# Edge stage of a four-layer tower: compares for the next one-hots ahead of the picking, softmax pieces behind it, fetched columns laid out place by place

## Chip, cores and metric
One Trainium2 chip, one of its cores. The metric is the device time of one launch in microseconds (us), median of several executions.

## The reference
The program is a tower of four layers over 16384 tokens of 64 features (float32). The change lies in the graph attention of layer 2, which the reference writes so:

```
h = (x_flat @ W_gat).reshape(M, HEADS, NUM_EXPERTS)        # M = 16384 nodes, 4 x 4 = 16 columns
a_src = (h * att_src).sum(-1)
a_dst = (h * att_dst).sum(-1)
e = leaky_relu(a_src[src] + a_dst[dst], negative_slope=0.2)  # 262144 edges and one loop per node
e_max = segment_max(e, dst)
ee = exp(e - e_max[dst])
denom = segment_sum(ee, dst)
msg = h[src] * (ee / denom[dst])[:, :, None]
agg = segment_sum(msg, dst) + b_gat
```

Everything else of the tower (embeddings, three other attentions, four expert layers) is the same in both kernels.

## The kernel before
The edges lie sorted by destination, 2048 to each of the 128 partitions. `edge_softmax` walks them in 32 chunks of 64 edges per partition and keeps a running softmax along each partition's row. For every edge it needs the 16 columns of `h[src]` and four logits. It gets them in two ways: 36 of the 64 edges of a chunk come by indirect DMA (POOL, L2875), and 28 are fetched by TensorE. These 28 are handled in 7 groups of 4 edges; one edge place on all 128 partitions is called a tile here.

A fetched group goes through four steps:

- **Compares** (`prepare`, DVE, L2961). Four `tensor_scalar` build a one-hot matrix for the group in `hot_room`, which has two slots. They read lanes that SP's queue loads ahead (`columns`, L2836).
- **Matmuls** (PE, `fetch`, L2887). Per tile 8 matmuls of 512 columns write one of 4 banks in PSUM. A tile waits until the bank's last content, 4 tiles earlier, was copied out (`fetched_in`). The 512 columns hold 32 candidate places times 16 channels.
- **Copy** (ACT, `take`, L2907). One copy per tile from the bank to `fetched` in SBUF, which has two slots, too. It waits until the slot's last group was picked (`selected`).
- **Picking** (`select`, DVE, L2978 to L2983). Five halvings by the low bits of the source: `copy_predicated` over 1024, 512, 256 and 128 elements, a copy and a last `copy_predicated` of 64.

Beside them each chunk has softmax pieces. `maxima` (DVE, L2989 to L3017) does the destination logits, the source logits of the fetched edges (a product into `inp_s`, L3002, and its sum, L3004), the running maximum and the differences. `exps` (ACT, L2912 to L2914) takes three exponentials of them. `sums` (DVE, L3021 to L3026) scales the values and runs the sums in one scan. `states` (ACT, L2920 to L2922) copies the chunk's results by time into `GT`, from where SP's queue stores them. `low_bits` (L2956) makes the masks for a whole chunk; before the change it stands inside `maxima`.

The order of the work is written out by hand, a loop of instructions per engine, with semaphores between engines. While chunk c has its softmax, the fetched groups of chunk c+1 pass. DVE's order for one chunk is: `maxima(c)`, `select` of group 0 of c+1, compares of group 2, `sums(c)`, then for groups 1 to 6 `select` and the compares two groups on. ACT's order is: copies of group 0, `exps(c)`, copies of groups 1 and 2, `states(c)`, copies of groups 3 to 6.

Of the kernel before, what the change touches and what calls it, by code (L numbers as in the profile page):

```python
# [2583 lines left out]
BLOCKS = 4  # L2584
# [193 lines left out]
def edge_softmax(nc, g, q, att_src):  # L2778
# [7 lines left out]
    with Stage(nc, "edges") as st:  # L2786
# [16 lines left out]
        parts = g.part_room[:].rearrange("p (s b c u) -> p s b c u", s=PARTS, b=BLOCKS, c=CH)  # L2803
        fetched = g.XT[:, TOKENS // 2:TOKENS // 2 + 2 * PER_GROUP * WIDE].rearrange(
            "p (s t c u) -> p s t c u", s=2, t=PER_GROUP, c=CH)
        whole = g.XT[:, TOKENS // 2:TOKENS // 2 + TILES * CH].rearrange("p (b c u) -> p b c u", b=BLOCKS, c=CH)
# [8 lines left out]
        (split, numbered, powers, att_in, hot_ready, bank_full, fetched_in, halved, selected, pe_passed, act_passed, dve_passed) = (  # L2815
            st.sem(n) for n in ("split", "numbered", "powers", "att_in", "hot_ready", "bank_full", "fetched_in", "halved", "selected",
                                "pe_passed", "act_passed", "dve_passed"))
# [5 lines left out]
        with nc.Block() as block:  # L2823
# [56 lines left out]
            def _(pe):  # L2880
                def fetch(n, j, k):
                    wait_apart(pe, hot_ready, n * GROUPS + j + 1, pe_passed)
                    for t in range(PER_GROUP):
                        pe.wait_ge(fetched_in, n * ON_PE + j * PER_GROUP + t + 1)
                        for b in range(BLOCKS):
                            for p in range(PARTS):
                                m = nc.tensor.matmul(banks[t % BANKS][:], hot[:, (k * GROUPS + j) % 2, b, t, :],  # L2887
                                                     parts[:, p, b].rearrange("p c u -> p (c u)"),
                                                     start=b == 0 and p == 0, stop=b == BLOCKS - 1 and p == PARTS - 1)
# [9 lines left out]
            def _(act):  # L2899
# [3 lines left out]
                def take(n, j, k):  # L2903
                    wait_apart(act, selected, n * GROUPS + j + 1, act_passed)
                    for t in range(PER_GROUP):
                        act.wait_ge(bank_full, n * ON_PE + j * PER_GROUP + t + 1)
                        nc.scalar.copy(fetched[:, (k * GROUPS + j) % 2, t].rearrange("p c u -> p (c u)"),  # L2907
# [36 lines left out]
            def _(v):  # L2944
# [26 lines left out]
                def select(n, j, k):  # L2971
                    at = fetched[:, (k * GROUPS + j) % 2]
                    to = rows[:, k, BY_DMA + j * PER_GROUP:BY_DMA + (j + 1) * PER_GROUP, 0:CH]
                    taken = lambda s, w: bc(bc(bits[:, s, j * PER_GROUP:(j + 1) * PER_GROUP], 2, CH), 3, w)
# [8 lines left out]
                    vec.copy_predicated(to, bc(bits[:, LOW_BITS - 1, j * PER_GROUP:(j + 1) * PER_GROUP], 2, CH),  # L2983
                                        at[:, :, :, 1]).then_inc(selected, 1)

                def maxima(c, k, i, more):
# [53 lines left out]
                low_bits(0).then_inc(cleared, 1)  # L3040
                values = q.table[:, :, 0:CH].rearrange("p (b u) c -> p b c u", b=BLOCKS)
# [14 lines left out]
                v.wait_ge(cleared, 6)  # L3056
# [3 lines left out]
                v.wait_ge(cleared, 7)  # L3060
                prepare(0, 0, 0)
                prepare(0, 1, 0)
                for j in range(GROUPS):
                    select(0, j, 0)
                    ahead(0, j, 0)
# [287 lines left out]
```

## Time and profile before

| | |
|---|---|
| median of 3 runs | 7020.88 us (7016.52 to 7023.06) |
| profiled execution, its own time | 7022.01 us |
| span of that execution | 7020.3 us |
| busy in the span: PE, DVE, ACT, POOL | 5579.5, 5269.5, 2713.2, 1967.5 us |
| PE matmuls of the edge stage (L2887) | 7168, busy 1709.6 us |
| DVE picking (L2978, four forms) | 896, busy 662.2 us |
| DVE compares (L2961) | 896, busy 380.4 us |
| ACT copies (L2907) | 896, busy 520.1 us |

The page gives the busy time of each engine over the whole program; the edge stage is only the part from about 3340 to 5235 us. What its engines do in turn is read from the timelines of one chunk, some 59 us long, since the same pattern comes 31 times. In a timeline a row starts with its time from the start of the span; idle time before it and who ended it stand in brackets.

### The profile page before, as it was taken

The numbers are of one execution on the slowest core, as the hardware profiler recorded it, in microseconds if no ns is written. First come the engines' busy times: TensorE is split into PE (matmuls) and PEld (weight loads), VectorE is DVE, ScalarE is ACT, GpSimd is POOL, SyncE is SP. The second block draws the span as 40 slices with busy tenths as digits, with TensorE's granted clock in tenths as the row PEclk, the third lists the DMA queues.
The fourth block names the chain that finished last, engine by engine and source line by source line (L and its number), as shares of the span: only waits on it lengthen the run. The fifth ranks groups of instructions, "written<-read, shape, count | busy, mean of one in ns | idle before, by whom it ended". The sixth has DMA issues, their size and how long they took to land. (4 is left out here: it accounts for less than half of the span.)

```text
span 7020.3 us, 109468 instructions
## 1 busy us (share of the span) xinstructions
PE 5579.5 (79%) x41602; PEld 3506.8 (50%) x41668; DVE 5269.5 (75%) x8911; ACT 2713.2 (39%) x4310; POOL 1967.5 (28%) x1937
## 2 busy tenths in 40 slices
PE   4659888958639999960899999999970689689998
PEld 3552256622126666650777777777750258523332
DVE  7869977878878888860778877887772667677776
ACT  3534433434336666640333333333330332233332
POOL 0010010010047800007766666666636010100000
PEclk8869999979869999975999999999985899799999
DMA  0000000011121000000221221111111000000001
GB/s 16 1 6 1 25 17 22 8 35 37 55 32 15 19 2 2 2 35 14 37 35 35 37 38 38 37 38 38 38 29 11 1 3 3 17 1 1 1 1 25
DMA packets 152249, 141.18 MB, mean 20 GB/s; under 512 B 71746, under 2 KB 136420, under 8 KB 150052
## 3 DMA queue, kind: packets, MB, share of 16 engines
q1 hardware_dynamic: 98462, 115.20, 5.8%
q0 software_dynamic: 53376, 20.06, 3.6%
q8 instruction: 277, 4.54, 0.3%
q14 instruction: 122, 0.99, 0.0%
q10 hardware_dynamic: 12, 0.39, 0.0%
HBM read 62.80 MB, written 38.09 MB: 14 GB/s over the span
## 5 line engine op out<-in xcount | busy, mean ns | idle before, releaser
L2887 PE MATMUL edges_bank<-part_room,hot_room 128*128 128x512 f32 x7168 | 1709.6, 401 | 370.6 <-DVE hot_room L2961 368.0
L2887 PEld LDWEIGHTS edges_bank<-part_room,hot_room 128*128 128x128 f32 x7168 | 1389.1, 195 | 691.0 <-issue 373.0
L2875 POOL DMA_INDIRECT XT<-gat_node_table,edges_idx x1152 | 1194.7, 1037 | 656.5 <-issue 342.8
L2907 ACT COPY XT<-edges_bank 128x512 f32<-128x512 f32 x896 | 520.1, 593 | 1191.4 <-PE edges_bank L2887 1190.6
L2978 DVE COPY_PREDICATED XT<-edges_tabs_p,XT 128x1024 f32<-128x1024 int32 (+3 forms) x896 | 662.2, 739 | 328.5 <-ACT XT L2907 298.1
L1005 ACT ACTIVATE expd_act_out<-expd_hp 128x1024 f32<-128x1024 f32 x256 | 262.2, 1024 | 527.1 <-PE expd_hp L927 527.1
L1041 DVE TENSOR_TENSOR expd_act_out<-expd_act_out,expd_h 128x1024 f32<-128x1024 f32 x256 | 312.6, 1221 | 186.5 <-ACT expd_act_out L1005 185.6
L1459 ACT ACTIVATE GT<-attc_sc,attc_nm 128x256 f32<-128x256 f32 x1024 | 400.4, 481 | 36.2 <-DVE attc_nm L1525 36.2
L1473 ACT ACTIVATE GT<-attc_sct 128x1024 f32<-128x1024 f32 x256 | 262.4, 1025 | 325.9 <-PE attc_sct L1393 325.3
L2961 DVE TENSOR_SCALAR hot_room<-edges_lanes,edges_nodes 128x512 fp32r<-128x512 f16 x896 | 380.4, 487 | 0.0
L1524 DVE TENSOR_REDUCE attc_mx<-attc_sc 128x4 f32<-128x1024 f32 x256 | 313.3, 1224 | 87.3 <-PE attc_sc L1382 87.2
L1382 PE MATMUL attc_sc<-XT,attc_tT 64*128 64x256 f32 x2048 | 296.4, 409 | 45.4 <-ACT GT L1459 45.4
L1046 DVE TENSOR_TENSOR expd_hid<-expd_act_out,expd_gp 128x1024 f32<-128x1024 f32 x256 | 312.5, 1221 | 8.8
L1529 DVE TENSOR_REDUCE attc_rs<-GT 128x4 f32<-128x1024 f32 x256 | 310.1, 1211 | 1.3 <-ACT GT L1459 1.3
L927 PE MATMUL expd_hp<-XT,expd_in_w 64*128 64x512 f32 x1024 | 289.0, 641 | 3.3 <-PEq L82 2.0
L1403 PE MATMUL attc_op<-GT,attc_xB 128*64 128x256 f32 x2048 | 277.5, 391 | 7.2 <-ACT GT L1480 2.0
L959 PE MATMUL expd_yp<-expd_hid,expd_in_w 128*64 128x512 f32 x1024 | 276.8, 619 | 1.6 <-DVE expd_hid L1046 1.6
L505 POOL TENSOR_TENSOR ln_f_xn<-H,ln_f_mean 128x1024 f32<-128x1024 f32 x4 | 11.4, 2846 | 947.5 <-DVE ln_f_shift L542 947.5
L1393 PE MATMUL attc_sct<-attc_tT,XT 64*128 64x256 f32 x2048 | 267.0, 378 | 1.6 <-DMA attc_tT<-attc_rT 1.0
L927 PE MATMUL expd_h<-XT,expd_in_wg 64*128 64x512 f32 x1024 | 263.3, 591 | 0.2 <-DVE expd_act_out L1041 0.2
L1382 PEld LDWEIGHTS attc_sc<-XT,attc_tT 64*128 64x128 f32 x2048 | 185.6, 190 | 144.6 <-issue 116.8
L798 PE MATMUL gates_gt<-identb,GT 128*128 128x128 bf16 x64 | 6.3, 266 | 262.5 <-DVE GT L789 261.2
(774 smaller groups left out, 9936.4 us busy)
## 6 DMA issues: line engine op xcount, KB each, us to landing
edges_lanes<-gat_places SPq DMA_DIRECT2D x224, 128.0 KB, 3.1
gat_states<-GT SPq DMA_DIRECT2D x32, 768.0 KB
XT<-gat_node_table,edges_idx POOLq DMA_INDIRECT x1152
XT<-XT SPq DMA_DIRECT2D x32, 256.0 KB
XT<-XT SPq DMA_DIRECT2D x64, 128.0 KB
XT<-XT SPq DMA_DIRECT2D x128, 64.0 KB
gat_starts<-nodes_zeros SPq DMA_DIRECT2D x4, 1088.0 KB, 7.9
attb_q<-attb_rows SPq DMA_DIRECT2D x256, 2.0 KB
```

Source lines behind the costliest of these rows:

```text
L927: m = nc.tensor.matmul(bank[:, odd, :], w[half, e, :], g.XT[half, i * U:(i + 1) * U], start=True, stop=True)
L1041: nc.vector.tensor_tensor(act_out[:, u % 2], act_out[:, u % 2], h2[:], ALU.mult).then_inc(product_ready, 1)
L1046: nc.vector.tensor_tensor(hid[:, u % 2], act_out[:, u % 2], gp[:], ALU.mult).then_inc(hid_full, 1)
L1382: m = nc.tensor.matmul(sc[(0, 1, 1, 0)[hp]][:, n, a * S:(a + 1) * S], tT[half, b % NB, hp, a * P:(a + 1) * P], x(b, half), start=True, sto ...
L1459: m = nc.scalar.activation(prob[:, hp % 2, n, a, :], sc[(0, 1, 1, 0)[hp]][:, n, a * S:(a + 1) * S], ACT.Exp, bias=nm[:, b % 2, n, hp, a:a ...
L1524: link(vec.tensor_reduce(best, sc[(0, 1, 1, 0)[hp]][:].rearrange("p n (a s) -> p n a s", s=S), AX.X, ALU.max))
L1529: vec.reduce_sum(rs[:, b % 2, :, hp, :], prob[:, hp % 2], AX.X).then_inc(totaled, 1)
L2875: nc.gpsimd.indirect_dma_start(out=rows[:, k, c, :], out_offset=None, in_=q.t_table, in_offset=bass.IndirectOffsetOnAxis(ap=idx[:, k, c:c ...
L2887: m = nc.tensor.matmul(banks[t % BANKS][:], hot[:, (k * GROUPS + j) % 2, b, t, :], parts[:, p, b].rearrange("p c u -> p (c u)"), start=b = ...
L2907: nc.scalar.copy(fetched[:, (k * GROUPS + j) % 2, t].rearrange("p c u -> p (c u)"), banks[t % BANKS][:]).then_inc(fetched_in, 1)
L2961: m = vec.tensor_scalar(hot[:, (k * GROUPS + j) % 2, b], lanes[:, j], nodes[:, b:b + 1], None, ALU.is_equal)
L2978: vec.copy_predicated(at[:, :, :, 0:w], taken(s, w), at[:, :, :, w:2 * w]).then_inc(halved, 1)
```

## The change
DVE's order for one chunk becomes: compares of group 2 of c+1, `low_bits(c+1)`, `select` of group 0, `maxima(c)`, compares of group 3, `select` of group 1, `sums(c)`, then compares ahead of `select` for groups 2 to 6. Compares now wait for PE's matmuls of the group that had the slot (`bank_full`), which the picking did for them before. `low_bits` gets a semaphore of its own and a wait on it. On ACT the copies of group 1 go ahead of `exps(c)`; `states(c)` stays behind the copies of group 2. The fetched columns, and the tables that PE multiplies by, are laid out place by place (u, then c) in place of channel by channel (c, then u), so that each halving reads and writes runs of w x 16 elements in place of w. The product of L3002 goes to a contiguous `prod` in place of `inp_s`. The clearing of `halved` moves behind the last `copy_predicated`.

```diff
-        fetched = ... "p (s t c u) -> p s t c u", s=2, t=PER_GROUP, c=CH)
+        fetched = ... "p (s t u c) -> p s t u c", s=2, t=PER_GROUP, c=CH)
...
+        prod = g.XT[:, at + 2 * HEADS2 * W:at + 2 * HEADS2 * W + ON_PE * CH].rearrange("p (t h e) -> p t h e", h=HEADS2, e=PERH)
...
                 def during(c, k, i):
                     take(c + 1, 0, 1 - k)
+                    take(c + 1, 1, 1 - k)
                     exps(c)
-                    take(c + 1, 1, 1 - k)
                     take(c + 1, 2, 1 - k)
                     states(c, k, i)
...
                 def low_bits(c):
                     at = src_row[:, ds(c * C + BY_DMA, ON_PE)]
-                    return vec.tensor_tensor(bits, bc(at, 1, LOW_BITS), bc(pow2[:], 2, ON_PE), ALU.bitwise_and)
+                    v.wait_ge(selected, c * GROUPS + 2)
+                    vec.tensor_tensor(bits, bc(at, 1, LOW_BITS), bc(pow2[:], 2, ON_PE), ALU.bitwise_and).then_inc(bits_ready, 1)
+                    v.wait_ge(bits_ready, c + 1)
 
                 def prepare(n, j, k):
+                    if not (isinstance(n, int) and n == 0 and j < 2):
+                        v.wait_ge(bank_full, n * ON_PE + (j - 1) * PER_GROUP)
                     v.wait_ge(lanes_in[j], 16 * n + 16)
...
-                        vec.copy_predicated(at[:, :, :, 0:w], taken(s, w), at[:, :, :, w:2 * w]).then_inc(halved, 1)
+                        vec.copy_predicated(half(0, w), taken(s, w), half(w, 2 * w)).then_inc(halved, 1)
                         v.wait_ge(halved, s + 1)
-                    vec.tensor_copy(to, at[:, :, :, 0]).then_inc(halved, 1)
+                    vec.tensor_copy(to, at[:, :, 0, :]).then_inc(halved, 1)
                     v.wait_ge(halved, LOW_BITS)
+                    vec.copy_predicated(to, taken(LOW_BITS - 1, 1), at[:, :, 1, :]).then_inc(selected, 1)
                     v.sem_clear(halved)
...
-                    if not (isinstance(c, int) and c == CHUNKS - 1):
-                        low_bits(c + 1)
                     values = rows[:, k, BY_DMA:, 0:CH]
-                    prod = inp_s[:, :, 1:, 1:1 + ON_PE].rearrange("p h e t -> p t h e")
...
                 def step(c, k, i, more):
                     last = isinstance(c, int) and c == CHUNKS - 1
-                    maxima(c, k, i, more)
-                    if not last:
-                        select(c + 1, 0, 1 - k)
-                        ahead(c + 1, 0, 1 - k)
-                    sums(c, k)
-                    if not last:
-                        for j in range(1, GROUPS):
+                    for j in range(GROUPS):
+                        if not last:
+                            ahead(c + 1, j, 1 - k)
+                            if j == 0:
+                                low_bits(c + 1)
                             select(c + 1, j, 1 - k)
-                            ahead(c + 1, j, 1 - k)
+                        if j == 0:
+                            maxima(c, k, i, more)
+                        if j == 1:
+                            sums(c, k)
```

Three lines of code are added ahead of these places, so a line of the kernel before has a number one to five lower than the same line after (the matmuls L2887 become L2888, the compares L2961 become L2966, the scan L3026 becomes L3028).

On DVE, at the head of a chunk, `maxima` ends with L3017, and the order before goes on so (L2978 to L2983 pick group 0, L2961 are the compares of group 2, L3021 begins `sums`; "ISA" and "REGISTER_ALU" rows are waits and their values):

```order
L3017 SCALAR_TENSOR_TENSOR XT<-XT,edges_tabs_p 128x256
L39 ISA
L2978 COPY_PREDICATED XT<-edges_tabs_p,XT 128x64x16
L2978 COPY_PREDICATED XT<-edges_tabs_p,XT 128x64x8
L2978 COPY_PREDICATED XT<-edges_tabs_p,XT 128x64x4
L2978 COPY_PREDICATED XT<-edges_tabs_p,XT 128x64x2
L2980 COPY XT<-XT 128x4x16
L2982 ISA
L2983 COPY_PREDICATED XT<-edges_tabs_p,XT 128x4x16
L2959 ISA
L2961 TENSOR_SCALAR hot_room<-edges_lanes,edges_nodes 128x512 x4
L3021 COPY edges_inp_s<-edges_acc_s 128x20
```

After the change the same end of `maxima` (now L3019) is followed by this (L2966 compares, L2984 to L2989 picking, L3023 begins `sums`):

```order
L3019 SCALAR_TENSOR_TENSOR XT<-XT,edges_tabs_p 128x256
L2966 TENSOR_SCALAR hot_room<-edges_lanes,edges_nodes 128x512 x4
L39 REGISTER_ALU
L2984 COPY_PREDICATED XT<-edges_tabs_p,XT 128x4x256
L2984 COPY_PREDICATED XT<-edges_tabs_p,XT 128x4x128
L2984 COPY_PREDICATED XT<-edges_tabs_p,XT 128x4x64
L2984 COPY_PREDICATED XT<-edges_tabs_p,XT 128x4x32
L2986 COPY XT<-XT 128x4x16
L2988 COPY_PREDICATED XT<-edges_tabs_p,XT 128x4x16
L2989 ISA
L3023 COPY edges_inp_s<-edges_acc_s 128x20
L3024 ISA
```

The picking of group 0 and the compares of group 2 are gone from between `maxima` and `sums` (they stand ahead of `maxima`), and the compares of group 3 and the picking of group 1 stand there now.

On ACT the place of `states` (L2921 to L2923, before L2920 to L2922) after the change is this; the copy under it is the first of group 3:

```order
L2918 ISA
L2921 COPY GT<-XT 128x4x64
L2922 COPY GT<-edges_acc_s 128x4x64
L2923 COPY GT<-edges_acc_s 128x16x64
L39 REGISTER_ALU
L2907 REGISTER_ALU
L2908 COPY XT<-edges_bank 128x512
```

Before the change the same seven rows stand there, with numbers one lower: `states(c)` is behind the copies of group 2 and ahead of those of group 3 in both.

## Rows read from the trace of the kernel before

**Rows 1.** Page and the matmul line's own view (line engine op | busy, mean ns | idle)
```profile
L2887 PE MATMUL edges_bank<-part_room,hot_room 128*128 128x512 f32 x7168 | 1709.6, 401 | 370.6 <-DVE hot_room L2961 368.0
...
L2887 PE MATMUL edges_bank<-part_room,hot_room x7168: 387/389/791, 3341.1 to 5227.9; 128*128 128x512 f32 x200
```

**Rows 2.** Timeline of PE: start us, us, engine line op count [idle before <-releaser]
```profile
3983.64 17.39 PE L2887 MATMUL edges_bank<-part_room,hot_room 128*128 128x512 f32 x76
4005.74 9.06 PE L2887 MATMUL edges_bank<-part_room,hot_room 128*128 128x512 f32 x32 [4.71 <-DVE hot_room L2961]
4016.50 43.83 PE L2887 MATMUL edges_bank<-part_room,hot_room 128*128 128x512 f32 x192 [1.70 <-DVE hot_room L2961]
4064.87 10.10 PE L2887 MATMUL edges_bank<-part_room,hot_room 128*128 128x512 f32 x32 [4.54 <-DVE hot_room L2961]
```

**Rows 3.** Timeline of DVE in this and the next chunk, columns as in rows 2
```profile
3987.29 3.06 DVE L2978 COPY_PREDICATED XT<-edges_tabs_p,XT 128x1024 f32<-128x1024 int32 x4 [1.75 <-ACT XT L2907]
...
3992.51 0.42 DVE L2989 TENSOR_SCALAR edges_tabs_p<-X 128x256 f32 x1
...
3994.56 0.31 DVE L2956 TENSOR_TENSOR edges_tabs_p<-X,edges_pow 128x140 int32<-128x140 int32 x1 [0.26 <-DVE edges_dst_p L2993]
3994.78 0.95 DVE L3002 TENSOR_TENSOR edges_inp_s<-XT,edges_tabs_p 128x448 f32<-128x448 f32 x1
...
4000.22 3.01 DVE L2978 COPY_PREDICATED XT<-edges_tabs_p,XT 128x1024 f32<-128x1024 int32 x4
...
4003.79 1.67 DVE L2961 TENSOR_SCALAR hot_room<-edges_lanes,edges_nodes 128x512 fp32r<-128x512 f16 x4
4005.37 0.18 DVE L3021 COPY edges_inp_s<-edges_acc_s 128x20 f32<-128x20 f32 x1
...
4010.86 3.08 DVE L2978 COPY_PREDICATED XT<-edges_tabs_p,XT 128x1024 f32<-128x1024 int32 x4 [0.23 <-DVE edges_acc_s L3026]
...
4014.52 1.67 DVE L2961 TENSOR_SCALAR hot_room<-edges_lanes,edges_nodes 128x512 fp32r<-128x512 f16 x4
...
4051.82 0.43 DVE L2989 TENSOR_SCALAR edges_tabs_p<-X 128x256 f32 x1
...
4059.34 1.30 DVE L2978 COPY_PREDICATED XT<-edges_tabs_p,XT 128x1024 f32<-128x1024 int32 x1
```

**Rows 4.** Timeline of ACT in the same chunk, columns as in rows 2
```profile
3993.81 0.59 ACT L2907 COPY XT<-edges_bank 128x512 f32<-128x512 f32 x1 [1.22 <-PE edges_bank L2887]
4000.34 0.39 ACT L2912 ACTIVATE edges_weights_p<-XT 128x256 f32<-128x256 f32 x1 [5.94 <-DVE XT L3017]
...
4002.13 2.03 ACT L2907 COPY XT<-edges_bank 128x512 f32<-128x512 f32 x4
...
4015.32 0.83 ACT L2920 COPY GT<-XT 128x256 f32<-128x256 f32 x1
...
4019.06 0.71 ACT L2907 COPY XT<-edges_bank 128x512 f32<-128x512 f32 x1
```

**Rows 5.** Windows: us, busy us of PE, PEld, DVE, ACT, POOL, PEclk, DMA, GB/s
```profile
4005.50:4009.00 3.50, 3.26 (x8) 2.59 (x9) 3.47 (x3) 0.00 (x0) 0.48 (x1) 0.51 0.14 37
4009.00:4045.00 36.00, 34.30 (x152) 28.02 (x151) 26.91 (x51) 14.94 (x22) 28.08 (x27) 1.00 0.24 44
```

**Rows 6.** Groups by form, DVE, edge stage (last: another stage): busy us, mean ns | idle
```profile
L2978 DVE COPY_PREDICATED XT<-edges_tabs_p,XT 128x128 f32<-128x128 int32 x224 | 102.0, 455 | 7.7
...
L2978 DVE COPY_PREDICATED XT<-edges_tabs_p,XT 128x256 f32<-128x256 int32 x224 | 101.7, 454 | 7.7
...
L3002 DVE TENSOR_TENSOR edges_inp_s<-XT,edges_tabs_p 128x448 f32<-128x448 f32 x32 | 30.8, 963 | 0.0
...
L3004 DVE TENSOR_REDUCE XT<-edges_inp_s 128x112 f32<-128x448 f32 x32 | 30.6, 957 | 1.1
...
L3015 DVE TENSOR_TENSOR XT<-XT 128x256 f32<-128x256 f32 x32 | 13.6, 426 | 1.1
...
L1529 DVE TENSOR_REDUCE attc_rs<-GT 128x4 f32<-128x1024 f32 x256 | 310.1, 1211 | 1.3 <-ACT GT L1459 1.3
```

More of the change, by code:

```diff
@@ L2802, in edge_softmax @@
         hot = g.hot_room[:].rearrange("p (s b t e) -> p s b t e", s=2, b=BLOCKS, t=PER_GROUP)
-        parts = g.part_room[:].rearrange("p (s b c u) -> p s b c u", s=PARTS, b=BLOCKS, c=CH)
+        parts = g.part_room[:].rearrange("p (s b u c) -> p s b u c", s=PARTS, b=BLOCKS, c=CH)
         fetched = g.XT[:, TOKENS // 2:TOKENS // 2 + 2 * PER_GROUP * WIDE].rearrange(
-            "p (s t c u) -> p s t c u", s=2, t=PER_GROUP, c=CH)
-        whole = g.XT[:, TOKENS // 2:TOKENS // 2 + TILES * CH].rearrange("p (b c u) -> p b c u", b=BLOCKS, c=CH)
+            "p (s t u c) -> p s t u c", s=2, t=PER_GROUP, c=CH)
+        whole = g.XT[:, TOKENS // 2:TOKENS // 2 + TILES * CH].rearrange("p (b u c) -> p b u c", b=BLOCKS, c=CH)
         at = TOKENS // 2 + 2 * PER_GROUP * WIDE
@@ L2814, in edge_softmax @@
         banks = [st.ps(f"bank{m}", [P, WIDE]) for m in range(BANKS)]
-        (split, numbered, powers, att_in, hot_ready, bank_full, fetched_in, halved, selected, pe_passed, act_passed, dve_passed) = (
+        (split, numbered, powers, att_in, hot_ready, bank_full, fetched_in, halved, selected, pe_passed, act_passed, dve_passed, bits_ready) = (
             st.sem(n) for n in ("split", "numbered", "powers", "att_in", "hot_ready", "bank_full", "fetched_in", "halved", "selected",
-                                "pe_passed", "act_passed", "dve_passed"))
+                                "pe_passed", "act_passed", "dve_passed", "bits_ready"))
         cleared, own, idx_ready, rows_used, passed, diff_ready, exped, sums_ready, state_ready, starts_used = (
@@ L2906, in take @@
                         act.wait_ge(bank_full, n * ON_PE + j * PER_GROUP + t + 1)
-                        nc.scalar.copy(fetched[:, (k * GROUPS + j) % 2, t].rearrange("p c u -> p (c u)"),
+                        nc.scalar.copy(fetched[:, (k * GROUPS + j) % 2, t].rearrange("p u c -> p (u c)"),
                                        banks[t % BANKS][:]).then_inc(fetched_in, 1)
@@ L2973, in select @@
                     to = rows[:, k, BY_DMA + j * PER_GROUP:BY_DMA + (j + 1) * PER_GROUP, 0:CH]
-                    taken = lambda s, w: bc(bc(bits[:, s, j * PER_GROUP:(j + 1) * PER_GROUP], 2, CH), 3, w)
+                    taken = lambda s, w: bc(bits[:, s, j * PER_GROUP:(j + 1) * PER_GROUP], 2, w * CH)
+                    half = lambda a, b: at[:, :, a:b, :].rearrange("p t u c -> p t (u c)")
                     wait_apart(v, fetched_in, n * ON_PE + (j + 1) * PER_GROUP + BANKS, dve_passed)
@@ L3039, in _ @@
                 v.wait_ge(powers, LOW_BITS)
-                low_bits(0).then_inc(cleared, 1)
-                values = q.table[:, :, 0:CH].rearrange("p (b u) c -> p b c u", b=BLOCKS)
+                low_bits(0)
+                values = q.table[:, :, 0:CH].rearrange("p (b u) c -> p b u c", b=BLOCKS)
                 for b in range(BLOCKS):
@@ L3055, in _ @@
                 v.wait_ge(numbered, 2)
-                v.wait_ge(cleared, 6)
+                v.wait_ge(cleared, 5)
                 v.wait_ge(split, 3)
@@ L3059, in _ @@
                 vec.tensor_copy(att_p, att[:]).then_inc(cleared, 1)
-                v.wait_ge(cleared, 7)
+                v.wait_ge(cleared, 6)
                 prepare(0, 0, 0)
@@ L3063, in _ @@
                 for j in range(GROUPS):
+                    ahead(0, j, 0)
                     select(0, j, 0)
-                    ahead(0, j, 0)
                 def step(c, k, i, more):
                     last = isinstance(c, int) and c == CHUNKS - 1
-                    maxima(c, k, i, more)
-                    if not last:
-                        select(c + 1, 0, 1 - k)
-                        ahead(c + 1, 0, 1 - k)
-                    sums(c, k)
-                    if not last:
-                        for j in range(1, GROUPS):
+                    for j in range(GROUPS):
[3 more added lines that the diff above has]
+                                low_bits(c + 1)
                             select(c + 1, j, 1 - k)
-                            ahead(c + 1, j, 1 - k)
+                        if j == 0:
+                            maxima(c, k, i, more)
+                        if j == 1:
+                            sums(c, k)
                 with v.Fori(0, NI - 1) as i:
```

4 lines of the change are left out of this document (1 added, 3 removed).

## Prediction

> **What bounds the kernel now.** I read the page first, then the timelines of PE, DVE and ACT over one chunk, then windows of the clock and the groups by form. The page says which engine carries the edge stage: PE's matmuls L2887 are busy 1709.6 us, and DVE's compares (L2961) end nearly all their waits [rows 1]. Those 368 us also hold the time before the stage's first matmul; what counts is the pattern inside. The first matmul starts at 3341.1 and the last at 5227.9, 1886.8 us for 32 chunks. Undisturbed, 32 matmuls (a group) take 43.83 / 6 = 7.30 us [rows 2] and a chunk of 7 groups 51.1 us. The first chunk has no softmax beside it, so the other 31 take (1886.8 - 51.1) / 31 = **59.2 us each**. So PE loses 8.1 us per chunk.
>
> The PE timeline shows where. It stands 4.71 us ahead of group 2 of the next chunk and 1.70 us ahead of group 3, both for compares [rows 2]. Group 2 then takes 9.06 us, 1.75 more than 7.30, and one chunk later 10.10, 2.80 more: the granted clock there is 0.51 [rows 5], that is mostly 1.2 GHz in place of 2.4, right after the idle. I take 2.3 us as the mean. After the idle of 1.70 there is no such loss.
>
> The DVE timeline shows the cause. From 3987.29 to 4014.52 DVE works without a pause: picking of the old chunk's last group, compares, `maxima` (3992.51 to 4000.22), picking of group 0, the compares of group 2 that PE stands for (3 us after PE had run dry), `sums`, picking of group 1, compares of group 3 [rows 3]. ACT has its work behind these: `exps` at 4000.34 right after `maxima`, `states` from 4015.32 to 4019.06, each ahead of copies that empty PE's banks [rows 4]. What ends last before PE's stalls is DVE's chain; ACT's `states` costs nothing now, since `sums` had ended at 4010.63, before ACT came to it.
>
> **What the change does to the chain.** I count from A, the moment when ACT begins the last copy of group 0 (3993.81 in the shown chunk [rows 4]). PE starts group 1 at about the same time. The compares of group 2 need only group 0's matmuls, so they no longer stand behind `maxima`: they are done 1.7 us after A, and PE's 4.71 us ahead of group 2 go. But `sums` now comes behind `maxima`, two compares and two pickings, and `states` waits for `sums` on ACT, ahead of the copies of group 3. A tile of group 4 needs the bank of the tile four earlier, so **group 4 can't start before `states` is done**. The terms of that chain:
>
> - Start of the compares: 0.05 us (ACT and DVE hear of the same last matmul).
> - Compares of group 2: 4003.79 to 4005.37, 1.6 [rows 3].
> - `low_bits`: 0.31 for the instruction, and its new wait like that of L3026 on itself, 0.23 [rows 3]: 0.55.
> - Picking of group 0: 4010.86 to 4014.52 is 3.66 [rows 3]. Off this go 0.1 for the layout and 0.1 for the clearing that no longer stands before the last `copy_predicated` (3.08 of the 3.66 are the four halvings; 0.58 hold the copy, the clearing and the start of the last; bounds 0 and 0.2). 3.45.
> - `maxima`: 7.71 here and 7.52 a chunk later [rows 3], 7.6. `low_bits` leaves it (3994.56 to 3994.78, 0.22). The product L3002 takes 963 ns and the sum L3004 957 ns for 448 elements [rows 6]. Contiguous rows give 426 ns for 256 and 1211 for 1024, 1.02 ns an element, so 622 for 448; L3002 also reads PSUM, for which I leave 70 ns. That is 0.27 and 0.33 off. 6.8.
> - Compares of group 3: 1.6. Picking of group 1: 3.45.
> - `sums` to the end of its scan: 4005.37 to 4010.63, 5.3 [rows 3].
> - ACT hears of it: 0.1. `states`: 4015.32 to 4019.06, 3.75. First copy of group 3: 0.6 [rows 4]. PE starts 0.3 later, as it does after the compares (4003.79 + 1.67 to 4005.74, [rows 2, 3]).
>
> Together **27.5 us** from A to the start of group 4. Without stalls it would start at 3 x 7.3 = 21.9. The 5.6 us show as two stalls: `exps` now ends at about A + 14.5 (`maxima` over at A + 12.4 to 12.6, then 4000.34 to 4002.13, 1.8, [rows 4]) and the copies of group 2 follow, so group 3 starts near 15.4, 0.8 late; group 4 then stands some 4.8 us. After such an idle the clock falls as before, 2.3 us, and now nothing covers this: before, 1.70 of idle at group 3 would only have been longer without it. To the next A there are four groups, 29.2 us. Period: 27.5 + 29.2 + 2.3 = 59.0 us, against 59.2. Times 31 chunks that is 6 us.
>
> **The other edits.** The layout: the halving of 128 elements (runs of 2) takes 455 ns, as long as that of 256 (454) [rows 6]. Its price with runs of 32 lies between 0.27 (the last one, of 64 elements) and 0.455; I take 0.35. For the other forms 0, bounds 0 and 0.1 together. Away from the chain, in groups 2 to 6, the savings are hidden, since DVE waits for ACT's copies there (1.75 us at 3987.29 [rows 3]); the same covers the new waits. On the chain each compare's new wait on a register value could cost 0 to 0.2 (a wait added can't gain); I take 0, since such values are worked out while the instruction before runs. PE and ACT read and write 512 contiguous columns in both layouts: 0. SP's queue and POOL: their triggers (compares of c+1, `starts_used`, `rows_used`) come later in the chunk by up to 13 us, but what they load is needed a chunk later, so 0. Setup and the tail: under 1 us less.
>
> The page "SBUF — State Buffer" of the Trainium skill, section "Door 1", says that SBUF has 16-byte lines, that at least two hits per line are needed for full bandwidth, and that each crossing to a new line otherwise pays. By that rule the halving with runs of 2 floats would pay nothing, and the gain of 0.1 would be nil, 0.2 per chunk on the chain and 6 us in all; the row of 455 ns speaks against it.
>
> **The sum.** Profiled execution 7022.0 us - 6 = 7016; the median lies 1 us below that execution, so 7015 us. A measurement of this kernel tells about 0.2% from no change, 14 us, which is 0.45 us per chunk; "the same" is 7007 to 7035.
>
> **Rivals.**
> - *Slower: the layout gives nothing and the waits cost.* All the cost of L3002 and L3004 may lie elsewhere than in the stride: then 0.6 comes back, 0.2 from the halvings, 0.2 from the clearing, and 0.2 for waits. The chain is 28.7, the period 60.2, the time 7015 + 1.2 x 31 = 7052 us. It decides from a chain of 28.15 on. For it: all of it sits on a chain that has no slack any more. Against it: 963 ns for 448 elements where 426 do for 256 [rows 6]. Chance 0.16. "VectorE: DVE Perf Modes" of the Trainium skill, section "Mode 1× (REGULAR) — the baseline", says that odd strides simply run at one result per cycle; by this the layout would give nothing and this rival would be right in its largest part. The 963 and 957 ns disagree.
> - *Faster by the layout.* Every halving gains (another 0.1 per picking), and the copies too, the clock loses the smaller 1.75: chain 27.2, period 58.2, time 6990 us. Chance 0.14.
> - *The clock stays up.* The idle is split in two, 0.8 and 4.8; if neither makes the clock fall, 2.3 x 31 = 71 us more go: 6944 us. For it: no fall at 1.70. Against: a fall at 4.54 and at 4.71 [rows 2, 5]. Chance 0.05.
> - *The change does all it says,* and `states` on ACT doesn't hold PE: group 4 then waits for its own compares only, scan end at A + 22.8, + 0.23 + 1.67 + 0.3 = 25.0, no fall of the clock, period 54.2, time 6860 us. Against it: the order of ACT, where `states` precedes the copies of group 3 before and after, with four banks. Chance 0.03.
>
> **Numbers.** The forecast, the stall traded for one of its size, has 0.62; the unknown terms spread it so that 0.15 of it lies under 7007, 0.05 above 7035. Faster: 0.15 + 0.14 + 0.05 + 0.03 = 0.37. Slower: 0.05 + 0.16 = 0.21. Same 0.42. The range leaves out the two last rivals and half of the first: 6985 to 7045.
>
> **What the profile after would show.** PE without idle ahead of group 2, about 0.8 us ahead of group 3 and 4.8 ahead of group 4, released by ACT's copy and no longer by compares, and the slow matmuls in group 4. `states` starting at once after the scan, with ACT idle before it. The product and the sum at 0.6 to 0.7 us, the halving of 128 at 0.35. A period of 59.0. I am wrong if group 4 starts before `states` ends, or if PE's longest idle is under 4 us.

## The result, and the profile after it

The change takes 7031.26 us (median of 20 runs, 7020.52 to 7040.35), the kernel before beside it 7020.55 (20 runs, 7014.51 to 7032.59): a ratio of 1.0015 [1.0008, 1.0022]. So it is some 11 us slower, where the forecast was 7015 us, 6 us faster; the measured time lies in the range of 6985 to 7045. A later repeat gave 1.0016 [1.0006, 1.0025]. The profiled execution took 7029.04 us with a span of 7027.3.

First the matmul line's own view after the change (its duration, its first and last start):

```profile
L2888 PE MATMUL edges_bank<-part_room,hot_room x7168: 387/389/796, 3337.4 to 5237.9; 128*128 128x512 f32 x200
```

By the working of the prediction this is a period of (5237.9 - 3337.4 - 51.1) / 31 = 59.66 us, against 59.2 before [rows 1] and 59.0 forecast. The timeline of PE shows that the chunks are no longer all alike (columns: start us, us, engine line op, count, [idle before <-releaser]):

```profile
3961.09 46.13 PE L2888 MATMUL edges_bank<-part_room,hot_room 128*128 128x512 f32 x192 [4.72 <-ACT XT L2908]
4010.74 9.00 PE L2888 MATMUL edges_bank<-part_room,hot_room 128*128 128x512 f32 x32 [3.52 <-ACT XT L2908]
4022.95 52.98 PE L2888 MATMUL edges_bank<-part_room,hot_room 128*128 128x512 f32 x224 [3.20 <-ACT XT L2908]
4080.66 46.09 PE L2888 MATMUL edges_bank<-part_room,hot_room 128*128 128x512 f32 x192 [4.73 <-ACT XT L2908]
4130.38 8.91 PE L2888 MATMUL edges_bank<-part_room,hot_room 128*128 128x512 f32 x32 [3.63 <-ACT XT L2908]
```

The two compare stalls of before [rows 2] are gone, as forecast: ACT's copies release every stall. One chunk (start of its group 4 at 4080.66, 57.71 us after the one before) has a single stall of 4.73, ahead of group 4. The next (4142.58, 61.92 us later) has two, 3.63 ahead of group 3 and 3.29 ahead of group 4, with slow matmuls behind both: 8.91 us for a group of 7.30, and 52.98 for seven groups of 51.1. The kernel's loop holds two chunks, so the bad chunk is the one at its end. The timeline of DVE in such a chunk shows where it starts:

```profile
3987.21 2.94 DVE L2984 COPY_PREDICATED XT<-edges_tabs_p,XT 128x1024 f32<-128x1024 int32 x4
...
3990.47 0.24 DVE L2988 COPY_PREDICATED XT<-edges_tabs_p,XT 128x64 f32<-128x64 int32 x1
3996.06 1.68 DVE L2966 TENSOR_SCALAR hot_room<-edges_lanes,edges_nodes 128x512 fp32r<-128x512 f16 x4 [5.35 <-issue]
...
4008.22 1.67 DVE L2966 TENSOR_SCALAR hot_room<-edges_lanes,edges_nodes 128x512 fp32r<-128x512 f16 x4
...
4015.49 2.87 DVE L3028 TENSOR_TENSOR_SCAN edges_acc_s<-edges_decay,edges_inp_s 128x1300 f32<-128x1300 f32 x1
```

And the timeline of ACT beside it:

```profile
3992.75 0.59 ACT L2908 COPY XT<-edges_bank 128x512 f32<-128x512 f32 x1 [1.23 <-PE edges_bank L2888]
...
4008.33 0.39 ACT L2913 ACTIVATE edges_weights_p<-XT 128x256 f32<-128x256 f32 x1 [7.75 <-DVE XT L3019]
...
4018.45 0.83 ACT L2921 COPY GT<-XT 128x256 f32<-128x256 f32 x1 [6.30 <-DVE edges_acc_s L3028]
...
4022.19 2.16 ACT L2908 COPY XT<-edges_bank 128x512 f32<-128x512 f32 x4
```

A, the last copy of group 0, is at 3992.75. By then group 0's matmuls are done and DVE has been free for 2 us, and yet the compares start at 3996.06, 3.3 us after A in place of 0.05. "issue" says that DVE waited for nothing that the profile shows. Everything behind hangs on these 3.3 us: `exps` at 4008.33, the scan, `states` at 4018.45, the copies of group 3 at 4022.19. The view of the waits (engine, line, releaser: us in total, times, longest) counts them:

```profile
DVE hot_room L2966 <- issue: 73.7, 14, 5.5
```

14 times, 5.3 us each: the loop's jumps back. The pages list two queues that bring instructions, q8 and q14. q8 brings 277 packets in both kernels; q14 does not bring the same. Before (queue: packets, MB, share of 16 engines):

```profile
q14 instruction: 122, 0.99, 0.0%
```

After:

```profile
q14 instruction: 191, 1.56, 0.1%
```

69 packets more, of 8 KB each (0.57 MB): five for each of the 14 jumps. Their times in the trace tie them to DVE: at each of the 14 jumps one packet starts some 6 us ahead of it, three start 1.0 to 1.3, 3.4 to 3.8 and 5.8 to 6.3 us behind it, and one 58 us behind it; before, no packet of q14 comes from 20 us ahead of such a jump to 100 us behind it. Between two jumps back the trace of DVE has 257 instructions before and 274 after, and the loop begins 8 instructions later. After the jump the next instruction comes at 2.8 to 3.0 us (before 0.3) and the third at 5.1 to 5.5 us (before 0.5). The first packet behind the jump has landed by 1.6 us and the second by 4.2, so each of the two instructions comes 1.2 to 1.5 us after a packet.

**The theory (A): the order itself is as forecast, and the loss is code that DVE must load again at each jump back, since its loop no longer stays loaded.** Rival (B): the pause is one of the new order, whatever the code's place. A second question beside it was what the layout and the order give apart, and a third whether `states` is what holds group 4.

### The profile page after: what moved, and what is told of

The parts are those of the page before. It is cut to its first block and busy times, and to the rows that moved or that the text cites. A ratio compares the mean times of both kernels' runs of the same rounds, so it can differ in the third digit from the quotient of the medians.

```text
span 7027.3 us, 109736 instructions
## 1 busy us (share of the span) xinstructions
PE 5600.6 (80%) x41602; PEld 3517.4 (50%) x41668; DVE 5207.7 (74%) x8911; ACT 2704.5 (38%) x4310; POOL 1972.8 (28%) x1937
## 5 line engine op out<-in xcount | busy, mean ns | idle before, releaser
L2888 PE MATMUL edges_bank<-part_room,hot_room 128*128 128x512 f32 x7168 | 1726.7, 404 | 364.3 <-DVE hot_room L2966 190.1
L2888 PEld LDWEIGHTS edges_bank<-part_room,hot_room 128*128 128x128 f32 x7168 | 1400.6, 196 | 690.4 <-ACT XT L2908 199.9
L2966 DVE TENSOR_SCALAR hot_room<-edges_lanes,edges_nodes 128x512 fp32r<-128x512 f16 x896 | 381.2, 487 | 394.7 <-PE edges_bank L2888 319.9
L2984 DVE COPY_PREDICATED XT<-edges_tabs_p,XT 128x1024 f32<-128x1024 int32 (+3 forms) x896 | 628.7, 702 | 37.3 <-DVE edges_tabs_p L2958 7.4
L1473 ACT ACTIVATE GT<-attc_sct 128x1024 f32<-128x1024 f32 x256 | 262.2, 1024 | 326.7 <-PE attc_sct L1393 326.5
L1393 PEld LDWEIGHTS attc_sct<-attc_tT,XT 64*128 64x128 f32 x2048 | 204.4, 188 | 21.1 <-DMA attc_tT<-attc_rT 1.9
```

Source lines behind the costliest of these rows:

```text
L1393: m = nc.tensor.matmul(sct[:, n, j * S:(j + 1) * S], x(b, half)[:, j * P:(j + 1) * P], tT[half, b % NB, hp, :], start=True, stop=True)
L2966: m = vec.tensor_scalar(hot[:, (k * GROUPS + j) % 2, b], lanes[:, j], nodes[:, b:b + 1], None, ALU.is_equal)
L2984: vec.copy_predicated(half(0, w), taken(s, w), half(w, 2 * w)).then_inc(halved, 1)
```

## Experiments on the code's place

Twelve of the runs fell on chips where the kernel before takes 8234 to 8250 us; there only ratios are compared, each to the kernel before on the same chip. The runs of this section are from chips where it takes 7019.

**The order as it is, with the loop elsewhere.** 96 waits that are long fulfilled are put ahead of DVE's loop, in the first chunk. They come out as 48 instructions and move the loop's code; nothing in the loop differs.

```
                 for j in range(GROUPS):
+                    if j in (4, 5):
+                        for _ in range(48):
+                            v.wait_ge(cleared, 6)
                     ahead(0, j, 0)
```

> The kernel after, with 96 waits that are already fulfilled (48 instructions) in the first chunk, ahead of DVE's loop, where DVE is idle anyway; the loop itself is unchanged, but begins 48 instructions later. Theory A (instruction loading: behind its loop's backward branch DVE stands 2.8 us and then 2.4 us for code, because the body of 274 instructions at its old place no longer stays loaded): the two pauses go, the compares of group 2 start right after group 0's matmuls in every chunk, all chunks take the 57.7 us that every second one has now (PE's starts of group 4, 4022.95 to 4080.66), 31 x 2.0 = 62 us less: 6969 us. Theory B (the pause is a wait for data, a lanes load of SP's queue or PE's count): nothing changes, 7031 us.

6982.73 us, 0.9948 [0.9934, 0.9962] of before; the repeat below gives 0.9951. Queue q14 is back at 121 packets. The timeline of PE, over three chunks:

```profile
3947.02 45.40 PE L2888 MATMUL edges_bank<-part_room,hot_room 128*128 128x512 f32 x192 [4.70 <-ACT XT L2908]
3992.74 7.56 PE L2888 MATMUL edges_bank<-part_room,hot_room 128*128 128x512 f32 x32 [0.32 <-ACT XT L2908]
4004.96 53.00 PE L2888 MATMUL edges_bank<-part_room,hot_room 128*128 128x512 f32 x224 [4.66 <-ACT XT L2908]
4062.71 45.79 PE L2888 MATMUL edges_bank<-part_room,hot_room 128*128 128x512 f32 x192 [4.75 <-ACT XT L2908]
```

The pause is gone, and B with it: the same order without it is 36 us faster than before. The expected time was missed by 14 us, since I had taken 57.7 us for every chunk, and they alternate between about 57.75 and 58.4. Against the change as it was, 48 us are gained: 14 pauses of 3.3 us make 46. The packets that this run lacks are those that the change has behind its jumps: in its trace none comes near one.

**The old order with a longer loop.** The kernel before, with 32 more instructions in DVE's loop (fulfilled waits again), its start where it was.

```
                         for j in range(1, GROUPS):
+                            if j in (4, 5) and not isinstance(c, int):
+                                for _ in range(16):
+                                    v.wait_ge(cleared, 7)
                             select(c + 1, j, 1 - k)
```

> The kernel before with 64 waits that are already fulfilled (32 instructions) inside DVE's loop, at groups 4 and 5, where DVE waits for ACT anyway: the body grows from 257 to 289 instructions at the same place. Theory A (instruction loading): DVE stands some 5 us behind the branch, ahead of maxima and so on the chain, in 15 chunks: 15 x 5 = 75 us more, 7096 us. Theory B (the waits themselves cost, or nothing does): 7021 to 7027 us, no pause at the branch.

7048.49 us, 1.0044 [1.003, 1.0058], and q14 at 191 packets, exactly as in the change. The size was missed: 30 us in place of 75. In this order four compares that were issued ahead of the jump still run behind it and cover 1.6 us of the first pause. The rest is 1.3 to 1.6 us of idle ahead of `maxima` and some 0.5 inside it. So DVE's chain is 2.0 us longer per jump in mean (PE's period there is 61.1 to 61.5 us in place of 59.3), and 14 times that is 28 of the 30 us. The timeline of DVE has the first part:

```profile
3998.32 1.67 DVE L2961 TENSOR_SCALAR hot_room<-edges_lanes,edges_nodes 128x512 fp32r<-128x512 f16 x4
4001.43 0.43 DVE L2989 TENSOR_SCALAR edges_tabs_p<-X 128x256 f32 x1 [1.45 <-issue]
```

Of the timeline of PE, one bad and one good chunk:

```profile
4015.00 8.97 PE L2887 MATMUL edges_bank<-part_room,hot_room 128*128 128x512 f32 x32 [6.58 <-DVE hot_room L2961]
...
4074.06 10.05 PE L2887 MATMUL edges_bank<-part_room,hot_room 128*128 128x512 f32 x32 [4.51 <-DVE hot_room L2961]
```

**The same longer loop, moved.** The 32 in the loop, and 48 instructions ahead of it as in the first run.

> The same as b_body, and 48 instructions ahead of the loop as in a_shift. If the place of the body decides whether it stays loaded: no pause, 7021 to 7027 us. If its size alone does (257 stays, 289 doesn't): as b_body, 7096 us.

7020.46 us, 1.0002 [0.9993, 1.0011], q14 at 121. So neither the 32 waits nor the 48 cost anything that shows; the loss of the run before was the reload alone. The same rows of PE:

```profile
4009.05 10.40 PE L2887 MATMUL edges_bank<-part_room,hot_room 128*128 128x512 f32 x32 [4.73 <-DVE hot_room L2961]
...
4068.13 9.95 PE L2887 MATMUL edges_bank<-part_room,hot_room 128*128 128x512 f32 x32 [4.53 <-DVE hot_room L2961]
```

Five kernels, then. From about the same place a loop of 257 instructions stays, and loops of 274 and of 289 reload; begun 48 instructions later, loops of 274 and of 289 stay. So both length and place count; what rule they follow beyond these five was not measured. The loss can be put into the old order and taken out of the new one.

The Trainium skill, page "Runtime: NRT & Kernel Launch", section "Instruction fetch mechanics", has the rule: an engine's instruction memory is filled in blocks, two of which form its window, and "A taken branch whose target isn't in the current 2-page window forces a DMA fetch of the target page before execution can continue". It gives 256 instructions, 16 KiB, a block. The trace agrees that the jump fetches and that place counts beside length. It shows packets of 8 KB on q14 and not 16; the first two behind the jump come with a pause each, of some 3 and 2.4 us, for which the page has no price.

**Both again.** The first run and the change itself, later, beside the kernel before at 7019.22 us.

> a_shift once more. If the kernel before takes 7020 us on this chip: 6983 us, ratio 0.995, as measured. If it takes 8240: the layout's 1.1 us a chunk lie on the chain up to group 4, which those chips run undisturbed (idle of 0.8 to 1.1 us ahead of group 3 and 4.9 ahead of group 4 without the layout): 34 us less than the 8198 of the old layout, 8164 us, ratio 0.991. If the layout's gain is hidden there: 0.995.

> The kernel after, unchanged, beside it. Code loading behind the branch costs 48 us against f_shift, as on the first chip: ratio to before 1.0015 if before takes 7020 us; if it takes 8240 us, 8212 us, 0.997, unless PE's long pauses cover DVE's: then equal to f_shift.

6983.28 us, 0.9951 [0.9937, 0.9965], and 7028.94 us, 1.0016 [1.0006, 1.0025]: both stand.

## Experiments on layout and order

**The layout alone.** The kernel before with columns laid out place by place and a contiguous `prod`; the order of before.

```
-        parts = g.part_room[:].rearrange("p (s b c u) -> p s b c u", s=PARTS, b=BLOCKS, c=CH)
+        parts = g.part_room[:].rearrange("p (s b u c) -> p s b u c", s=PARTS, b=BLOCKS, c=CH)
...
-                        vec.copy_predicated(at[:, :, :, 0:w], taken(s, w), at[:, :, :, w:2 * w]).then_inc(halved, 1)
+                        vec.copy_predicated(half(0, w), taken(s, w), half(w, 2 * w)).then_inc(halved, 1)
...
-                    prod = inp_s[:, :, 1:, 1:1 + ON_PE].rearrange("p h e t -> p t h e")
```

> The kernel before, its order of work untouched, with the layout place by place and the contiguous product alone. Theory A (the layout's gains are real and lie on the chain of before, which runs through maxima and three pickings): 0.6 us for product and sum, 0.2 for each of three pickings, 1.2 to 1.3 us a chunk, 31 times: 6981 us. Theory B (what DVE saves is hidden or goes into idle of PE elsewhere): 7021 us.

6984.77 us, 0.9952 [0.9939, 0.9966]. The timeline of PE:

```profile
3984.59 9.13 PE L2888 MATMUL edges_bank<-part_room,hot_room 128*128 128x512 f32 x32 [3.68 <-DVE hot_room L2962]
3995.32 43.82 PE L2888 MATMUL edges_bank<-part_room,hot_room 128*128 128x512 f32 x192 [1.60 <-DVE hot_room L2962]
```

In the old order the chain up to the compares of group 2 is `maxima` and one picking, and the stall shrinks from 4.5 to 4.7 [rows 2] to 3.5 to 3.7. This is 34 us, about as much as all of the change gives without the reload (36). So the new order, beside this layout, gives nothing that these runs can tell.

**The order alone** (the first run with the old layout and the old `prod`), **`states` one group later,** and **both that and the compares of group 4 ahead of `sums`.** The edits, each upon the first run's kernel:

```
                     take(c + 1, 2, 1 - k)
+                    take(c + 1, 3, 1 - k)
                     states(c, k, i)
-                    for j in range(3, GROUPS):
+                    for j in range(4, GROUPS):
```

and for the last, in `step`, with the compares of group 4 taken from the place at j = 2:

```
                         if j == 1:
+                            if not last:
+                                ahead(c + 1, 2, 1 - k)
                             sums(c, k)
```

> a_shift (6983 us) with the old layout: columns channel by channel and the product into inp_s; the order of work of the change alone, with its code loaded. Theory A (the trade of the prediction: PE's stall moves from group 2 to group 4 and is about as long, and the layout shortens the new chain by 0.6 us in maxima and 0.2 to 0.3 in each of two pickings): 1.1 us x 31 = 34 us more, 7017 us, the same as before (7019). Theory B (the order gained by itself): near 6983. Theory C (the order loses by itself, the layout hides it): over 7030.

> a_shift with one line of ACT moved: states(c) stands behind the copies of group 3 and no longer ahead of them. Theory A (states holds PE through the banks): PE's idle of 4.7 us ahead of group 4 shrinks to some 2 us, now released by the compares of group 4 (scan end + 1.6), the clock doesn't fall behind so short an idle (2.0 us more): 4.6 x 31 = 143 us less, 6840 us. Theory B (the compares behind sums hold PE just as long): 6983 us.

> a_shift_states4, and on DVE the compares of group 4 ahead of sums (c) in place of behind it. Theory A: nothing on DVE or ACT is late for PE any more; DVE's work of some 46 us a chunk fits into PE's 51; a chunk takes 51.1 us in place of 58.1, 31 x 7 = 217 us less than a_shift: 6766 us, the edge stage bound by PE at full clock. Theory B (POOL's gathers, 36 a chunk at 1.04 us plus their issue, some 48 us, or the loads behind them become the bound): 6780 to 6850, with DVE waiting for gathered rows.

> The same as a_shift_best without the 48 instructions ahead of the loop, so the body stands where it does in the kernel after. Theory A (code loading again, two pauses of 5.2 us in all at the branch, of which 3.3 delay the compares of every second chunk): the compares of group 3 come 2.3 us late in every second chunk: 15 x 2.3 = 35 us or more over a_shift_best, 6800 us. Theory B (now covered by slack): equal to a_shift_best.

Of before (8249.67 us): 0.9962 [0.995, 0.9974] for the order alone, 0.9854 [0.9838, 0.9871] with `states` later, 0.9798 [0.9782, 0.9814] with both, and 0.9846 [0.9832, 0.9861] for both without the 48 instructions ahead of the loop (q14 at 191 again). They were measured again, to have them beside a kernel before at 7020 us, but the chips were of the slow kind each time (before: 8239.70, 8235.39 and 8233.97 us):

> a_shift_oldlayout once more, since the chip of its first run took 8250 us for the kernel before, with DVE waiting up to 36 us for the lanes loads, and says little of the chain. Theory A (the order alone trades one stall for another): 7017 us, ratio to before 1.000. Theory B (the order gained by itself): near 6983, 0.995. Theory C (it loses by itself): over 7030, 1.002 or more.

> a_shift_states4 once more, for the same reason. Theory A (states holds PE through the banks): PE's idle ahead of group 4 shrinks from 4.7 to some 2 us and the clock stays up: 6840 us, ratio to before 0.975. Theory B (the compares behind sums hold PE as long): 6983 us, 0.995.

> a_shift_best once more, for the same reason. Theory A (PE no longer waits for DVE or ACT): a chunk of 51.1 us, 6766 us, ratio 0.964. Theory B (POOL's gathers or the loads become the bound): 6780 to 6850.

> a_best_noshift once more. Theory A (code loading delays the compares of every second chunk by 3.3 us, 2.3 beyond the slack): 6800 us. Theory B (covered by slack): equal to c_best.

> a_shift_oldlayout on a chip where the kernel before takes 7020 us, if this one is such a one. Theory A (the order alone trades one stall for another, as forecast): 7017 us, ratio to before 1.000. Theory B (the order gained by itself): near 6983, 0.995, as the ratios of the two slow chips say. Theory C (it loses by itself): over 7030, 1.002 or more.

> a_shift_states4 beside it. Theory A (states holds PE through the banks, and no clock fall behind the 2 us of idle that stay): 6840 us, ratio 0.975. Theory B (the compares behind sums hold PE as long): 6983 us, 0.995.

> a_shift_best beside it. Theory A (PE no longer waits for DVE or ACT): 51.1 us a chunk, 6766 us, ratio 0.964. Theory B (POOL's gathers or the loads become the bound): 6780 to 6850.

> The order of the change alone, with its code loaded, once more on another chip. If the kernel before takes 7020 us there: Theory A (one stall for another) 7017 us, ratio 1.000; Theory B (the order gained by itself) near 6983, 0.995; Theory C (it loses) over 7030. If it takes 8240 us: 0.995 again, which says only that PE's own long pauses hide part of the chain there.

| | first series | second | third | fourth |
|---|---|---|---|---|
| order alone | 0.9962 | 0.9953 | 0.9954 | 0.9953 |
| `states` later | 0.9854 | 0.9797 | 0.9799 | |
| both | 0.9798 | 0.9744 | 0.9743 | |
| both, loop not moved | 0.9846 | 0.9755 | | |

Each has an interval of some 0.0015 to either side; the first series lies beyond that from the others in its last three rows, and why is open. What slows these chips lies elsewhere in the program and, in this stage, in group 6 and at the start of the next chunk: PE stands there for up to 19 us and waits for nothing that the profile shows, while DVE and ACT stand too (26.7 and 19.0 us in the chunk shown) for what the profile puts down to a DMA. From group 1 to the start of group 5 every chunk but the first runs undisturbed, so the rows there can be read. They are of the third series. PE in the order alone:

```profile
4504.44 7.56 PE L2887 MATMUL edges_bank<-part_room,hot_room 128*128 128x512 f32 x32 [0.84 <-ACT XT L2907]
4516.88 17.27 PE L2887 MATMUL edges_bank<-part_room,hot_room 128*128 128x512 f32 x64 [4.88 <-ACT XT L2907]
4551.21 3.78 PE L2887 MATMUL edges_bank<-part_room,hot_room 128*128 128x512 f32 x8 [17.06 <-issue]
```

PE with `states` behind the copies of group 3:

```profile
4547.61 7.55 PE L2888 MATMUL edges_bank<-part_room,hot_room 128*128 128x512 f32 x32 [0.28 <-ACT XT L2908]
4557.39 16.61 PE L2888 MATMUL edges_bank<-part_room,hot_room 128*128 128x512 f32 x72 [2.22 <-DVE hot_room L2967]
...
4811.29 18.25 PE L2888 MATMUL edges_bank<-part_room,hot_room 128*128 128x512 f32 x72 [2.23 <-DVE hot_room L2967]
```

PE with both:

```profile
4540.49 14.80 PE L2888 MATMUL edges_bank<-part_room,hot_room 128*128 128x512 f32 x64 [0.28 <-ACT XT L2908]
4555.63 11.19 PE L2888 MATMUL edges_bank<-part_room,hot_room 128*128 128x512 f32 x48 [0.34 <-DVE hot_room L2967]
```

With `states` moved by one group, the copy no longer ends the stall of group 4; the compares do, which stand behind `sums`, and 2.2 us are left. With the compares ahead of `sums` too, group 4 starts without idle (the 64 matmuls are groups 3 and 4), and 0.3 is left ahead of group 5. So `states` ahead of the copies of group 3 is what held PE, and the compares behind `sums` are what comes next. After 4.88 the clock falls (64 matmuls in 17.27 us). After 2.22 it stays up in the first row (72 in 16.61, as fast as elsewhere) and falls in the second (72 in 18.25, with 0.57 granted in its first 4 us). Over the three traces with `states` later the stall of group 4 is 2.1 to 2.3 us in all 93 chunks; in 26 the next 32 matmuls take 7.5 us and in 67 about 9.1.

Both together is faster than before in each of the three series, by 2.0 to 2.6%, and faster than the order alone by 1.6 to 2.1%. The last three kernels have the new layout and the order alone has the old one, and the first run's kernel was never measured on these chips; so these ratios don't part what the layout gives from what the moves give, and only the rows speak for the moves. Whether both together gain as much where the kernel before takes 7020 us was not measured; nor was the order alone there. By its rows the order alone loses 0.84 + 4.88 + (17.27 - 14.6) = 8.4 us in the chunk shown and 8.7 in mean over the chunks of four traces, against 8.1 before: by estimate 19 us more in all, where these chips show 0.4 to 0.5% less. No profile shows the kernel before on such a chip, so that stays open, as does the cause of the long pauses. In the same measure the first run's kernel loses 7.1 us: by estimate the layout takes 1.6 us a chunk off the new chain, and took 1.1 (34 us in all) off the old. Moving the loop is worth 0.0048 in the first series and 0.0011, within the intervals, in the second: there its size is not settled, while q14 shows the reload both times.

## Why the prediction was wrong

**The step that failed** is in the part on the other edits: "On the chain each compare's new wait on a register value could cost 0 to 0.2 (a wait added can't gain); I take 0". It counts the added instructions by what each does, and no term, bound or rival holds what they do together to DVE's loop: 257 instructions became 274, the loop began 8 later, and the jump back, free before, cost 5.3 us of DVE, 3.3 us on the chain, in 14 chunks. That is 46 us by rows and 48 by the runs (7031 against 6983; 46 in the repeat). Without it the time is 6983, under the forecast and just below the range's lower end of 6985. That the time falls into the range is luck: a gain that was forecast too small and a loss that was left out meet there.

**The trade of stalls was right, and the chain nearly.** The timeline of DVE in the first run's kernel, with the loop moved, has each term:

```profile
3978.06 1.68 DVE L2966 TENSOR_SCALAR hot_room<-edges_lanes,edges_nodes 128x512 fp32r<-128x512 f16 x4 [2.36 <-PE edges_bank L2888]
3979.66 0.30 DVE L2958 TENSOR_TENSOR edges_tabs_p<-X,edges_pow 128x140 int32<-128x140 int32 x1
3980.20 2.94 DVE L2984 COPY_PREDICATED XT<-edges_tabs_p,XT 128x1024 f32<-128x1024 int32 x4 [0.24 <-DVE edges_tabs_p L2958]
...
3983.64 0.43 DVE L2994 TENSOR_SCALAR edges_tabs_p<-X 128x256 f32 x1
...
3990.21 1.67 DVE L2966 TENSOR_SCALAR hot_room<-edges_lanes,edges_nodes 128x512 fp32r<-128x512 f16 x4
3991.80 2.91 DVE L2984 COPY_PREDICATED XT<-edges_tabs_p,XT 128x1024 f32<-128x1024 int32 x4
...
3995.11 0.18 DVE L3023 COPY edges_inp_s<-edges_acc_s 128x20 f32<-128x20 f32 x1
```

And the timeline of ACT its ends:

```profile
3977.96 0.59 ACT L2908 COPY XT<-edges_bank 128x512 f32<-128x512 f32 x1 [1.22 <-PE edges_bank L2888]
...
4000.47 0.83 ACT L2921 COPY GT<-XT 128x256 f32<-128x256 f32 x1 [6.31 <-DVE edges_acc_s L3028]
...
4004.21 2.15 ACT L2908 COPY XT<-edges_bank 128x512 f32<-128x512 f32 x4
```

| term | forecast | measured |
|---|---|---|
| start, compares of group 2 | 0.05, 1.6 | 0.10, 1.60 |
| `low_bits` | 0.55 | 0.54 |
| picking of group 0 | 3.45 | 3.44 |
| `maxima` | 6.8 | 6.57 |
| compares of group 3 | 1.6 | 1.59 |
| picking of group 1 | 3.45 | 3.31 |
| `sums` and ACT's start | 5.4 | 5.36 |
| `states` | 3.75 | 3.74 |
| to group 4 | 0.9 | 0.75 |
| together | 27.5 | 27.0 |

Half a microsecond less of chain, and 1.9 us for the clock's fall (53.00 against 51.1) in place of 2.3: 7.0 us lost per chunk where 7.9 were forecast, which is 28 of the 32 us between 7015 and 6983. Both sizes matter only because nothing covers the chain any more, as the text said.

**The signs named.** PE without idle ahead of group 2: right in the good chunks; at the loop's end the pause ahead of its compares still comes out as the longer stall of group 3. 0.8 ahead of group 3: 0.32 without the reload, 3.5 with it. 4.8 ahead of group 4, released by ACT's copy: 4.7, and 3.2 in the bad chunks. `states` at once after the scan with ACT idle before it: right (6.30). Period 59.0: 59.66. Neither of the two signs of being wrong came: group 4 starts after `states`, and PE's longest idle is 4.9 us. They watched the chain between the stalls, and the loss lies ahead of it.

**The layout.** The groups by form of the change, DVE (line engine op, form, count | busy us, mean ns | idle):

```profile
L2984 DVE COPY_PREDICATED XT<-edges_tabs_p,XT 128x1024 f32<-128x1024 int32 x224 | 294.6, 1315 | 14.2 <-DVE edges_tabs_p L2958 7.4 <-ACT XT L2908 6.8
...
L2984 DVE COPY_PREDICATED XT<-edges_tabs_p,XT 128x256 f32<-128x256 int32 x224 | 100.7, 450 | 7.7
L2984 DVE COPY_PREDICATED XT<-edges_tabs_p,XT 128x128 f32<-128x128 int32 x224 | 68.0, 304 | 7.7
...
L3004 DVE TENSOR_TENSOR XT<-XT,edges_tabs_p 128x448 f32<-128x448 f32 x32 | 19.9, 621 | 1.1
L3006 DVE TENSOR_REDUCE XT<-XT 128x112 f32<-128x448 f32 x32 | 19.8, 620 | 1.1
```

The product takes 621 ns (forecast 690), so the 70 ns that I left for reading PSUM don't exist; the sum 620 (622). The halving of 128 elements takes 304 (350), that of 256 the same 450 as before. The layout's rule of the Trainium skill ("SBUF — State Buffer", "Door 1"), by which runs of two floats pay nothing, does not agree with 455 against 304 ns for the same elements; nor does, for strides as long as these, that of "VectorE: DVE Perf Modes", section "Mode 1× (REGULAR) — the baseline", of the Trainium skill with 963 against 621. The mask's access pattern and the product's place changed together with the stride, and no run parts them.

**The rivals.** Slower by no gain of the layout and by costly waits: the side was right, the mechanism not, since the layout gives 34 us by itself and 32 instructions added to the loop cost nothing in the moved kernel. Faster by the layout, 6990 us, is nearest to what the change gives without the reload: its chain of 27.2 and its clock loss of 1.75 are near the measured 27.0 and 1.9. Its reasons are only in part those: the halving of 256 elements gained nothing and that of 1024 lost, and the layout alone leaves ACT's copies at 592 ns (before 593); the largest part of the chain's half microsecond is `maxima`. The clock fell, and `states` held PE, as argued against the last two.

## What to carry to other kernels

When an edit adds instructions to an engine's loop, or ahead of it, compare the packets of that engine's instruction queue before and after, and look at the first instructions behind the jump back: a pause there that is put down to issue, together with more such packets, was code being loaded here, and it depended on the loop's place as well as on its length. Try the same kernel with the loop moved before judging the edit, since a real gain of 0.5% can hide behind it. And when a wait is taken from one engine's chain, ask at once which step of another engine then stands ahead of the buffer's release: here moving `states` by one group took 2.5 us of PE's idle per chunk (4.7 to 2.2 by rows), where the whole change, without the reload, gains 36 us or 1.2 per chunk. That the 2.5 us come out in the time of a chip at 7020 us was not measured.

## What had not been expected of the hardware

- With nearly the same code (257 instructions against 274) the third instruction behind a jump back in DVE's loop comes 0.5 us or 5.3 us later, and a longer loop (289) is free again 48 instructions further on. PE's loop of 982 instructions and ACT's of 158 never pause at theirs: PE's next instruction comes 0.11 us later, ACT's 0.24.
- The clock also fell after every idle of 3.0 to 3.7 us (9.00 and 9.13 us for a group of 7.30), and after none of 1.3 to 1.9, in the traces of the change and its repeat, the layout alone, the kernel before and the old order with the longer loop. After idles of 2.2 us it fell in 67 of 93 chunks.
- The new layout made the largest halving, of 1024 elements, slower rather than faster: 1315 ns, against 1274 ns in the order alone, which has the old layout; and 1331 ns in the layout alone, against 1289 before.
